# Five projections of an attention block, each cut in two halves around the first half of the next step's scores

## The reference

```python
h = layernorm(xn) * ln1_g + ln1_b
q, k, v = heads(h @ WQ + bQ), heads(h @ WK + bK), heads(h @ WV + bV)    # 16 heads of 8
scores = einsum('bhqd,bhkd->bhqk', q, k) / sqrt(8)                      # allowed: 0 <= i - j < 128
attn_out = (softmax(scores) @ v) @ WO + bO
s_t = A * s_(t-1) + (h @ Bw)_t                                          # 64 states, a scan over the tokens
g = sigmoid(h @ Wg + bg)
x1 = xn + g * attn_out + (1 - g) * (s @ Cw)
s = x1 + gelu(layernorm(x1) @ W1 + b1) @ W2 + b2
f = silu(mixture of 8 experts, top 2, of xn)
out = x + s * f
```

## Time and profile before

| | |
|---|---|
| median of 3 timed runs | 944.48 us |
| profiled execution, its own time | 946.94 us |
| its span | 945.20 us |
| TensorE busy | 844.1 us (89%) |
| VectorE busy | 718.8 us (76%) |
| ScalarE busy | 723.5 us (77%) |
| GpSimd busy | 485.2 us (51%) |
| mean granted TensorE clock | 0.975 of full speed |

### The profile page before, as it was taken

The page is one execution under the profiler, slowest core; times in us unless marked ns, Lnnn a source line. Parts: engine busy times, 40 slices in busy tenths (PEclk is TensorE's granted clock), DMA queues, the critical chain, the costliest instruction groups (busy, mean ns, idle before and its releaser), DMA issues.

```text
span 945.2 us, 37694 instructions
## 1 busy us (share of the span) xinstructions
PE 844.1 (89%) x15720; PEld 541.6 (57%) x15768; DVE 718.8 (76%) x1785; ACT 723.5 (77%) x1251; POOL 485.2 (51%) x786
## 2 busy tenths in 40 slices
PE   3569899999999999999999999999999999988987
PEld 2345655647565665756566575656657565664645
DVE  7567868879787787888778787878878787776535
ACT  5337787878788788888778788877888887776775
POOL 6417345382735548173653817365481736444262
PEclk9758999999999999999999999999999999999999
DMA  5942516132341614234261423426143242610101
GB/s 133 219 76 82 72 51 129 55 100 42 118 75 60 132 54 108 46 109 72 69 123 53 108 45 109 73 70 121 54 106 46 102 72 69 111 43 7 30 2 35
DMA packets 85597, 75.14 MB, mean 79 GB/s; under 512 B 9457, under 2 KB 79154, under 8 KB 85426
## 3 DMA queue, kind: packets, MB, share of 16 engines
q1 hardware_dynamic: 83346, 71.93, 34.0%
q10 hardware_dynamic: 2080, 0.79, 0.3%
HBM read 36.26 MB, written 30.15 MB: 70 GB/s over the span
## 4 chain that ended last, share of the span: by engine, by line
PE 63%; DVE 15%; ACT 9%; issue 7%; POOL 2%; DMA 2%; SPq 1%; POOLq 0%; DVEq 0%; ACTq 0%
PE ps L569 12%; PE ps L511 8%; PE ps L834 6%; PE ps L797 5%; PE ps L500 4%; PE ps L786 3%; DVE mx L1212 3%; PE ps L588 3%; DVE gc L1339 3%; DVE act_t L1359 2%; PE ps L526 2%; ACT lin L1024 2%; PE ps L727 2%; PE ps L583 2%; ACT ga L1028 2%
## 5 line engine op out<-in xcount | busy, mean ns | idle before, releaser
L1212 DVE TENSOR_REDUCE mx<-ps 128x2 f32<-128x320 f32 (+1 forms) x512 | 219.0, 467 | 114.6 <-PE ps L526 113.9
L994 ACT ACTIVATE pt<-ps 128x1024 f32<-128x1024 f32 (+1 forms) x256 | 233.5, 916 | 60.0 <-PE ps L500 56.6
L1478 POOL TENSOR_SCALAR_AFFINE_SELECT pt<-pt 128x512 f32<-128x512 f32 x256 | 162.5, 638 | 153.9 <-ACT pt L994 151.9
L511 PE MATMUL ps<-kd,qz 48*32 48x160 bf16 (+1 forms) x4096 | 147.7, 237 | 21.1 <-DVE mx L1212 11.5
L500 PE MATMUL ps<-qz,kd 51*32 51x256 bf16 (+1 forms) x4096 | 157.0, 262 | 1.6 <-ACT pt L994 1.0
L786 PEld LDWEIGHTS ps<-m,act_t 128*128 128x128 f32 x1024 | 126.7, 191 | 47.8 <-DVE act_t L1359 36.3
L786 PE MATMUL ps<-m,act_t 128*128 128x128 f32 x1024 | 143.3, 283 | 10.8 <-DVE act_t L1359 8.8
L569 PE MATMUL ps<-pt,va 128*32 128x256 f32 (+1 forms) x2048 | 149.3, 366 | 2.7 <-POOL pt L1481 1.2
L511 PEld LDWEIGHTS ps<-kd,qz 48*32 48x32 bf16 x4096 | 76.9, 91 | 120.4 <-issue 67.2
L1481 POOL TENSOR_SCALAR_AFFINE_SELECT pt<-pt 128x512 f32<-128x512 f32 x192 | 122.2, 637 | 0.0
L1024 ACT ACTIVATE lin<-ps,mbias 128x512 f32<-128x512 f32 x128 | 87.4, 683 | 36.6 <-DVE act_t L1359 18.8
(11 more groups left out here) (187 smaller groups left out, 1619.1 us busy)
## 6 DMA issues: line engine op xcount, KB each, us to landing
qz<-qk_parts SPq DMA_DIRECT2D x32, 384.0 KB, 6.7
kd<-qk_parts SPq DMA_DIRECT2D x32, 384.0 KB, 10.1
qk_parts<-qp SPq DMA_DIRECT2D x16, 384.0 KB, 3.1
qk_parts<-kp SPq DMA_DIRECT2D x16, 384.0 KB, 2.8
xl<-L_attn_x SPq DMA_DIRECT2D x16, 256.0 KB, 3.7
qk_parts<-qp SPq DMA_DIRECT2D x16, 256.0 KB, 3.1
qk_parts<-kp SPq DMA_DIRECT2D x16, 256.0 KB, 2.9
xnr<-xn SPq DMA_DIRECT2D x16, 256.0 KB, 2.5
```

The source lines that it names most:

```text
L511: nc.tensor.matmul(ps[QG * c:QG * (c + 1), 4 + par, w * pr:w * (pr + 1)], qz[q][rows, 2 * g + pr, P * i + QG * c:P * i + QG * (c + 1)], kd ...
L994: nc.scalar.activation(to, src, ACT.Exp, scale=SCALE).then_inc(exp_ok.sem, 1)
L1212: nc.vector.tensor_reduce(mx[:, i, HG * g + pr:HG * (g + 1):2], src, AX.X, ALU.max).then_inc(mx_ok.sem, 1)
L1478: sel1 = nc.gpsimd.affine_select(out=pt[:, s, :, 0:P], in_=pt[:, s, :, 0:P], compare_op=ALU.is_ge, fill=0.0, base=0, pattern=[[0, HG], [1, ...
```

## The change

Each `project_x` is now a `begin_x`, which holds the waits, the bias matmul of v and g, and the first half of the columns, and a second part, `part_x(m, 1)`, which does the other half and signals. In the loop the first half stays where the projection was, behind the values of step n. The second half stands in step n + 1 between the two halves of the scores. In the prologue the two halves follow each other. The orders of the other engines and the number of signals stay as they are.

```diff
+            def part_q(m, s):
+                cols_ = slice(T // 2 * s, T // 2 * (s + 1))
+                mm = nc.tensor.matmul(bank(bank_of(m, "q"))[:, cols_], wq[:], turned(m)[:, cols_], start=True, stop=True, skip_group_check=True)
+                if s:
+                    mm.then_inc(q_ps.sem, 1)
+
+            def begin_q(m):
                 pe.wait_ge(*done(hT_ok, m))
                 if m == 1:
                     pe.wait_ge(*done(qkr_ok, 0, 1))
-                nc.tensor.matmul(bank(bank_of(m, "q")), wq[:], turned(m)[:], start=True, stop=True).then_inc(q_ps.sem, 1)
+                part_q(m, 0)
+
+            def project_q(m):
+                begin_q(m)
+                part_q(m, 1)
...
+            def part_v(m, s):
+                for t in (2 * s, 2 * s + 1):
+                    mm = nc.tensor.matmul(bank_t(bank_of(m, "v"))[:, t], turned(m)[:, P * t:P * (t + 1)], wv[:], start=False, stop=True, skip_group_check=True)
+                if s:
+                    mm.then_inc(v_ps.sem, 1)
+
+            def begin_v(m):
...
                 add_bias(k, 0)
-                for t in range(NT):
-                    mm = nc.tensor.matmul(bank_t(k)[:, t], turned(m)[:, P * t:P * (t + 1)], wv[:], start=False, stop=True, skip_group_check=True)
-                mm.then_inc(v_ps.sem, 1)
+                part_v(m, 0)
...
+            SECOND = {AT_Q + 1: part_q, AT_K + 1: part_k, AT_U + 1: part_u, AT_V + 1: part_v, AT_G + 1: part_g}
+
             def body(b, q):
...
                     if n < NCH:
                         scores(b, q, n, 0)
+                        if nx2 and n in SECOND:
+                            SECOND[n](b + 2, 1)
                         scores(b, q, n, 1)
...
                         if n == AT_Q:
-                            project_q(b + 2)
+                            begin_q(b + 2)
```

More of the change, by code:

```diff
@@ L594, in turn_h0 @@
                 turn4(bank(bank_of(m, "h")), lambda t: h0[:, t]).then_inc(hT_ps.sem, 1)
-            def project_q(m):
+            def part_q(m, s):
[4 more added lines that the diff above has]
+            def begin_q(m):
                 pe.wait_ge(*done(hT_ok, m))
@@ L599, in project_q @@
                     pe.wait_ge(*done(qkr_ok, 0, 1))
-                nc.tensor.matmul(bank(bank_of(m, "q")), wq[:], turned(m)[:], start=True, stop=True).then_inc(q_ps.sem, 1)
-            def project_k(m):
-                pe.wait_ge(*(done(qkr_ok, m, 1) if m >= 2 else done(qkr_ok, m - 1, 2)))
-                nc.tensor.matmul(bank(bank_of(m, "k")), wk[:], turned(m)[:], start=True, stop=True).then_inc(k_ps.sem, 1)
+                part_q(m, 0)
+            def project_q(m):
+                begin_q(m)
+                part_q(m, 1)
@@ new lines, in part_k, with begin_k @@
+            def part_k(m, s):
+                cols_ = slice(T // 2 * s, T // 2 * (s + 1))
+                mm = nc.tensor.matmul(bank(bank_of(m, "k"))[:, cols_], wk[:], turned(m)[:, cols_], start=True, stop=True, skip_group_check=True)
+                if s:
+                    mm.then_inc(k_ps.sem, 1)
+            def begin_k(m):
+                pe.wait_ge(*(done(qkr_ok, m, 1) if m >= 2 else done(qkr_ok, m - 1, 2)))
+                part_k(m, 0)
+            def project_k(m):
+                begin_k(m)
+                part_k(m, 1)
@@ L606, in project_u, with part_u, begin_u @@
+            def part_u(m, s):
+                cols_ = slice(T // 2 * s, T // 2 * (s + 1))
+                mm = nc.tensor.matmul(bank(bank_of(m, "u"))[:, cols_], bw[:], turned(m)[:, cols_], start=True, stop=True, skip_group_check=True)
+                if s:
+                    mm.then_inc(u_ps.sem, 1)
+            def begin_u(m):
+                pe.wait_ge(*(done(qkr_ok, m, 2) if m >= 2 else done(st_ok, m - 1)))
+                part_u(m, 0)
             def project_u(m):
-                pe.wait_ge(*(done(qkr_ok, m, 2) if m >= 2 else done(st_ok, m - 1)))
@@ L608, in project_u @@
-                nc.tensor.matmul(bank(bank_of(m, "u")), bw[:], turned(m)[:], start=True, stop=True).then_inc(u_ps.sem, 1)
+                begin_u(m)
+                part_u(m, 1)
             def add_bias(k, n):
                 nc.tensor.matmul(bank_t(k), onesb[0:65], bias3[0:65, n].unsqueeze(1).to_broadcast([65, NT, P]), start=True, stop=False, skip_group_check=True)
-            def project_v(m):
+            def part_v(m, s):
+                for t in (2 * s, 2 * s + 1):
+                    mm = nc.tensor.matmul(bank_t(bank_of(m, "v"))[:, t], turned(m)[:, P * t:P * (t + 1)], wv[:], start=False, stop=True, skip_group_check=True)
+                if s:
+                    mm.then_inc(v_ps.sem, 1)
@@ L619, in project_v, with part_g, begin_g @@
                 add_bias(k, 0)
-                for t in range(NT):
-                    mm = nc.tensor.matmul(bank_t(k)[:, t], turned(m)[:, P * t:P * (t + 1)], wv[:], start=False, stop=True, skip_group_check=True)
-                mm.then_inc(v_ps.sem, 1)
-            def project_g(m):
+                part_v(m, 0)
+            def project_v(m):
+                begin_v(m)
+                part_v(m, 1)
+            def part_g(m, s):
+                for t in (2 * s, 2 * s + 1):
+                    mm = nc.tensor.matmul(bank_t(bank_of(m, "g"))[:, t], turned(m)[:, P * t:P * (t + 1)], wg[:], start=False, stop=True, skip_group_check=True)
+                if s:
+                    mm.then_inc(g_ps.sem, 1)
+            def begin_g(m):
                 k = bank_of(m, "g")
@@ L628, in project_g @@
                 add_bias(k, 1)
-                for t in range(NT):
-                    mm = nc.tensor.matmul(bank_t(k)[:, t], turned(m)[:, P * t:P * (t + 1)], wg[:], start=False, stop=True, skip_group_check=True)
-                mm.then_inc(g_ps.sem, 1)
+                part_g(m, 0)
+            def project_g(m):
+                begin_g(m)
+                part_g(m, 1)
             def turn_nf(m):
@@ L759, in body @@
                         if n == AT_Q:
-                            project_q(b + 2)
+                            begin_q(b + 2)
                         if n == AT_K:
-                            project_k(b + 2)
+                            begin_k(b + 2)
                         if n == AT_U:
-                            project_u(b + 2)
+                            begin_u(b + 2)
                         if n == AT_V:
-                            project_v(b + 2)
+                            begin_v(b + 2)
                         if n == AT_G:
-                            project_g(b + 2)
+                            begin_g(b + 2)
                     if nxt and n == AT_C:
```

## The result

The changed kernel takes 963.46 us (median of 4 runs, 959.31 to 963.91); the kernel before took 943.83 us (943.18 to 944.85), now with 4 runs. The ratio is 1.0197, 95% interval 1.0167 to 1.0228: slower by 2.0%. The profiled execution took 963.06 us with a span of 961.3 us.

What follows compares the result with a forecast made beforehand. TensorE was taken to set the loop's pace; 3 x 0.15 + 0.12 + 0.26 = 0.83 us a batch, over 14 batches 11.6 us, gave 956 us. Range 945 to 965, the forecast's own 952 to 961.

Steps and rivals of the forecast that it cites:

- rival C: Late evictions make TensorE wait at step 9's selection or `v_in`, 0.5 us a batch: 7 us more, 963; chance 0.18.
- What bounds the loop: In the 16-step loop TensorE sets the pace, busy 23.55 of 24.70 us; VectorE mostly waits for it.
- Smaller passes cost nothing: In q, k and u, two more passes and weight loads each are hidden inside a half: 0.
- A visit costs 0.26: Each second half between scores costs TensorE 0.20 + 0.06 us beside its columns, five per batch; bounds 0 to 0.35.
- 0.11 given back in steps 6, 8, 14: Second scores after q, k and g no longer wait for a maximum: 0.11 us back, net +0.15 each.
- u's visit mostly covered by the scan's wait: Ahead of v's bias matmul, the old wait for the scan covers the rest; u's share about +0.12 us.
- v +0.26: v's visit costs +0.26 us with nothing back; the turn of the attention output, waiting for `v_in`, is just covered.
- Nothing new at the end: From the turn of the combine weights to that of the maxima, forecast addition 0.
- Rival A: Faster: the half fits between scores at its columns' price, 0.44 us a batch given back, 6 us, 938.3; chance 0.11.
- B: No change: issue gaps, about 0.5 us a batch, and the scan's 0.35 nearly cover 0.83; 944 to 946, chance 0.09.

Runs made afterwards that it cites:

- e1: Changed kernel with all five projections still halved, but both halves together where the whole projection stood; ratio 1.0026 to the kernel before.
- e7: Kernel before with only u cut, its second half between the two halves of the scores of step 9; ratio 1.0070.
- e5: Changed kernel with each second half behind both halves of the next step's scores, ahead of the values; ratio 1.0206 to the kernel before.
- e2: Kernel before with only v cut, its second half between the two halves of the scores of step 11; ratio 1.0092.
- e6: Kernel before with only u cut, its second half behind both halves of the scores of step 9, ahead of the values; ratio 1.0033.
- e8: Kernel before, nothing cut, with v, the first turn of the attention output and g each one step later; ratio 1.0132.
- e3: Kernel before with only q, k and g cut, second halves between the score halves of steps 5, 7 and 13; ratio 1.0135.
- e4: Kernel before with q, k and g whole, moved between the two halves of the next step's scores; ratio 1.0108.
- e11: Kernel before, unchanged, profiled a second time; one run, 950.73 us.
- e9: As e8, with VectorE's scan also moved behind the second maximum of step 10 instead of step 9; ratio 1.0101 to the kernel before.

## Why the prediction was right, and where its sizes were off

Forecast 956 (945 to 965), slower with 0.80; measured 963.46. The direction and the mechanism held: TensorE pays for each added visit. The rise was 19.6 us for 11.6. The range held only by the part that had been booked for rival C: the forecast's own ended at 961, with a visit of 0.33. And C had put down 963, the measured number, but from waits of 0.5 us for late evictions that this kernel does not have; that C's number was the nearer one is luck.

- **What bounds the loop: right.** The added time in the stretch is TensorE busy, and the waits are the same two.
- **Smaller passes cost nothing: right**, e1.
- **A visit costs 0.26: too little, 0.35.** The 0.20 beside the columns came out to the hundredth. The way out of the scores was put at 0.06 from the states at the start of the batch and is 0.10; there the scores are of another shape (128 instead of 160 columns), and the row was not the nearest after all. And the second half of scores that starts alone costs 0.05 more up to the values than one that follows another half: in the earlier trace rows that stands as 0.34 for 0.30 behind a held half, and I had booked it as given back without booking it as paid. 0.09 x 5 x 14 = 6.3 us, less the part of u's that the wait ahead of v took.
- **0.11 given back in steps 6, 8, 14: right** (0.24 and 0.30 in step 6).
- **u's visit mostly covered by the scan's wait: right** in its size (0.14, or 0.17 against most iterations, for 0.12), and e7 has it alone at 0.15. Two figures in its working are off without effect: u would start at 360.07, not 360.09, and by the prediction's own terms TensorE would be ready for the bias matmul at 363.48, not 363.4 (363.03 without the wait, 0.30 from q and k, 0.15 from u). With 363.48 the wait left is 0.32, which is what was measured.
- **v +0.26: 0.35**, the bare price of a visit; the turn did not wait, as reckoned. e5 shows how near it was: 0.25 us later and it waits 0.31.
- **Nothing new at the end: wrong.** The prediction had no term behind g. The turn of the maxima comes 0.17 late beside the rest, and TensorE's weight loads wait for `nm` 8.1 us in all for 5.8. 14 x 0.17 = 2.4 us. The cause is in the two selections above, late by g's late eviction (GpSimd had been idle for 1.38 us until ScalarE's exponential, and that stood behind the eviction of g): VectorE's first `nm` instruction ends with the selection then running and takes 0.63 us for 0.44. e2, e6, e7 and e8, in which g stays a whole behind the values, don't have it (0.44 us in most iterations, 3.28 to 3.31 us for the stretch); e3 and e4, with g late and u and v as before, do (0.64 and 3.50). e5's stretch is 3.56 with 0.39 for that instruction, so there something else is late.
- **Rival A** (a free visit) is out by the trace. **B** (the waits take it) is out, save for u. What was said against it, that a gap of "issue" keeps its length wherever it falls, does not hold: in e11 the gaps stand at the same places in other lengths. **C** did not decide this kernel, but e4 and e5 show that each of its three places becomes a wait when the cover is gone; its condition, 0.4 to 0.5 us later, was set too high: 0.25 suffices.

What the Trainium skill, "TensorE: Matmul & The Clock Gate", Step-by-step, was cited for against the sum (weight loads pulled ahead, so that a stream costs its columns) did not hold at this border: the load of the second half's weights starts with its pass again, at 189.31 after scores that had started at 188.97.

## What to carry to other kernels

Count the visits of TensorE to another shape of tile before the matmuls: here each added one cost 0.35 us with the same columns, and five of them, less what came back, added 1.3 us to a batch of 55. Splitting work to fill another engine's idle time gains only what TensorE itself waited (0.11 here), and where an eviction stands in an in-order queue ahead of what the next step needs, a quarter of a microsecond of lateness can come back as three waits (e5). For changes near 5 us compare the quickest iterations as well as the times, and look into iterations that the change does not touch: here gaps that move with the length of the program were of that size.

## Not expected

One half of scores takes 0.24 us up to another half that follows, 0.30 up to the values when it follows another half, and 0.34 to 0.35 standing alone. So two halves that follow each other take 0.15 us less than two that are parted; which of their matmuls overlap is open.

The same VectorE instruction on 64 elements a partition takes 0.44 or 0.63 us, as GpSimd's selection beside it ends. And the VectorE scan of 512 columns (1.13 us to the next instruction) costs TensorE 0.35 where it stands; at the two other places tried, e8 and e9, TensorE paid 0.8 us, and 0.41 in the quickest iteration and 0.63 in the median, elsewhere.
